# Two column-half scatter chains in place of one row scatter chain, in an attention and mixture-of-experts kernel

## The reference, cut to what matters

```python
buf_tok = jnp.full((E, CAP), T, jnp.int32).at[sorted_e, pos].set(sorted_tok, mode='drop')  # E=64, CAP=128
gx = xp[buf_tok]                                          # up to 128 tokens for each expert
gu = jnp.einsum('ech,ehi->eci', gx, gate_up_proj)         # 512 -> 2*192
g, u = jnp.split(gu, 2, axis=-1)
hid = jax.nn.silu(g) * u
eo = jnp.einsum('eci,eih->ech', hid, down_proj) * buf_w[..., None]   # 192 -> 512
routed = jnp.zeros((T + 1, h), x.dtype).at[buf_tok.reshape(-1)].add(eo.reshape(-1, h))[:T]
shared = jax.nn.silu(xf @ shared_gate_w.T) * (xf @ shared_up_w.T) @ shared_down_w.T
x = x + routed + shared
```

## Times and profile before

| quantity | us |
|---|---|
| time, median of 3 runs | 708.5 |
| lowest and highest of them | 704.78, 715.64 |
| time of the profiled execution | 706.73 |
| span of its profile, first to last instruction | 705.0 |
| TensorE matmul busy | 584.1 |
| VectorE busy | 230.0 |
| POOL busy | 246.5 |

### The profile page before, as it was taken

The page is one execution under the profiler, slowest core; times in us unless marked ns, Lnnn a source line. Parts: engine busy times, 40 slices in busy tenths (PEclk is TensorE's granted clock), DMA queues, the critical chain, the costliest instruction groups (busy, mean ns, idle before and its releaser), DMA issues.

```text
span 705.0 us, 6326 instructions
## 1 busy us (share of the span) xinstructions
PE 584.1 (83%) x2035; PEld 312.2 (44%) x2035; DVE 230.0 (33%) x572; ACT 173.0 (25%) x352; POOL 246.5 (35%) x235
## 2 busy tenths in 40 slices
PE   5999827777799999999999997999789998964810
PEld 2444314554445555555555553555345554532400
DVE  3866724863832222222132221222212222220210
ACT  4577733365101111121111111111011121110100
POOL 1145573353141333343323424333233333324220
PEclk9999959778989999999999999999979999996965
DMA  8935434489134989999998897997968898987432
GB/s 231 242 131 105 42 109 158 170 257 280 60 108 132 272 222 272 251 268 268 248 263 230 223 261 202 263 262 218 255 158 252 245 269 267 241 208 198 101 45 34
DMA packets 68953, 141.44 MB, mean 201 GB/s; under 512 B 13553, under 2 KB 16113, under 8 KB 68913
## 3 DMA queue, kind: packets, MB, share of 16 engines
q1 hardware_dynamic: 48240, 93.22, 42.7%
q0 software_dynamic: 18032, 43.54, 30.2%
q10 hardware_dynamic: 2640, 4.20, 1.7%
HBM read 107.89 MB, written 33.04 MB: 200 GB/s over the span
## 4 chain that ended last, share of the span: by engine, by line
DMA 43%; PE 28%; issue 12%; DVE 5%; ACT 4%; POOL 4%; SPq 1%; POOLq 0%; ACTq 0%; DVEq 0%
DMA out<-y,table 38%; PE bank L773 8%; PE bank L652 6%; PE bank L761 5%; DMA out<-x 5%; PE bank L666 3%; PE bank L575 2%; ACT rows L844 1%; PE bank L753 1%; SPq L319 1%; POOL picked L416 1%; DVE ones_lo L1082 1%; POOL x L425 1%; DVE ones_hi L1078 1%; DVE s L1003 1%
## 5 line engine op out<-in xcount | busy, mean ns | idle before, releaser
L501 POOL DMA_INDIRECT out<-y,table x64 | 101.4, 1584 | 294.8 <-DMA out<-y,table 213.2
L773 PE MATMUL bank<-gu_w,gxT 128*128 128x384 f32 x512 | 176.6, 488 | 0.8 <-ACT gxT L945 0.8
L761 PE MATMUL bank<-dn_w,hidT 96*128 96x512 f32 x256 | 126.7, 618 | 1.0 <-DVE hidT L1216 1.0
L1199 DVE TENSOR_SCALAR y<-bank,gx 128x512 f32<-128x512 f32 x64 | 48.1, 751 | 225.1 <-PE bank L761 208.9
L773 PEld LDWEIGHTS bank<-gu_w,gxT 128*128 128x128 f32 x512 | 93.0, 192 | 52.2 <-issue 1.6
L953 ACT ACTIVATE eg<-bank 128x192 f32<-128x192 f32 x64 | 21.2, 331 | 287.5 <-PE bank L773 287.5
L652 PE MATMUL bank<-xnT,upT 128*128 128x512 f32 x192 | 91.3, 620 | 0.0
L1211 DVE TENSOR_TENSOR hid<-bank,eg 128x192 f32<-128x192 f32 x64 | 31.8, 497 | 130.1 <-ACT eg L953 130.1
L753 PE MATMUL bank<-ident,gx 128*128 128x128 f32 x256 | 40.9, 284 | 36.9 <-DMA gx<-rows_dram,table 36.9
L507 POOL DMA_INDIRECT gx<-rows_dram,table x64 | 63.6, 994 | 21.7 <-issue 18.9
L761 PEld LDWEIGHTS bank<-dn_w,hidT 96*128 96x128 f32 x256 | 47.7, 197 | 48.5 <-issue 47.1
(11 more groups left out here) (164 smaller groups left out, 464.9 us busy)
## 6 DMA issues: line engine op xcount, KB each, us to landing
gu_w<-in_gate_up SPq DMA_DIRECT2D x128, 384.0 KB, 4.3
dn_w<-in_down SPq DMA_DIRECT2D x128, 192.0 KB, 5.8
x<-in_x SPq DMA_DIRECT2D x4, 1024.0 KB, 9.3
feat_dram<-feat SPq DMA_DIRECT2D x16, 256.0 KB, 3.1
rows_dram<-rows ACTq DMA_DIRECT2D x4, 1024.0 KB, 4.8
out<-x SPq DMA_DIRECT2D x4, 1024.0 KB, 5.7
out<-x POOLq DMA_DIRECT2D x3, 1024.0 KB, 10.4
w<-in_W SPq DMA_DIRECT2D x5, 256.0 KB, 7.7
```

What stands on the lines that cost most here:

```text
L501: pool.indirect_dma_start(a["out"][:, :], bass.IndirectOffsetOnAxis(ap=table[:, e:e + 1], axis=0), y[:, e % YB, :], None, compute_op=ALU.a ...
L761: last = nc.tensor.matmul(DN[:], hidT[:, e % 2, j, :], dn_w[:, e % U, j, :], start=(j == 0), stop=(j == 1))
L773: last = nc.tensor.matmul(GU[e % 2][:, 0:2 * I], gxT[:, e % 2, c, :], gu_w[:, e % U, c, :], start=(c == 0), stop=(c == KC - 1))
L1199: nc.vector.tensor_scalar(y[:, e % YB, :], DN[:], gx[:, e % GX, D + e:D + e + 1], None, ALU.mult).then_inc(y_ready, 1)
```

## The change

The output is viewed as 4096 rows of 256 columns, so that row 2t is the left half of token t and row 2t+1 the right half. Each expert's scatter becomes two, `scatter(e, 0)` and `scatter(e, 1)`, with 128 rows of 256 columns each. Each half has a semaphore of its own, so the left halves wait only for left halves and the right ones for right ones. The three `add_shared` wait for both halves, and both halves wait for them. The addresses of the halves are made on VectorE beside `table`.

```diff
-                def scatter(e):
+                def scatter(e, h):
                     pool.wait_ge(y_ready, e + 1)
-                    if chain_before(e):
-                        pool.wait_ge(added, 16 * chain_before(e))
-                    pool.indirect_dma_start(a["out"][:, :], bass.IndirectOffsetOnAxis(ap=table[:, e:e + 1], axis=0),
-                                            y[:, e % YB, :], None, compute_op=ALU.add).then_inc(added, 16)
+                    if e:
+                        pool.wait_ge(half_added[h], 16 * e)
+                    if shared_before(e):
+                        pool.wait_ge(shared_added, 16 * shared_before(e))
+                    pool.indirect_dma_start(halves, bass.IndirectOffsetOnAxis(ap=half_at[:, h, e:e + 1], axis=0),
+                                            y[:, e % YB, h * (D // 2):(h + 1) * (D // 2)], None,
+                                            compute_op=ALU.add).then_inc(half_added[h], 16)
...
                 for e in range(E):
-                    scatter(e)
+                    scatter(e, 0)
+                    scatter(e, 1)
                     if e + GX < E:
                         gather(e + GX)
-                    if e + 1 < E and chain_before(e + 1) > chain_before(e) + 1:
-                        pool.wait_ge(added, 16 * (chain_before(e) + 1))
-                        add_shared(chain_before(e + 1) - (e + 1))
+                    if e + 1 < E and shared_before(e + 1) > shared_before(e):
+                        for h in range(2):
+                            pool.wait_ge(half_added[h], 16 * (e + 1))
+                        add_shared(shared_before(e + 1))
...
-                nc.vector.scalar_tensor_tensor(table[:], spare2[:], -1.0, POS[:, LIST], ALU.add, ALU.add).then_inc(table_ready, 1)
+                link(nc.vector.scalar_tensor_tensor(token_of[:], spare2[:], -1.0, POS[:, LIST], ALU.add, ALU.add))
+                nc.vector.tensor_copy(table[:], token_of[:]).then_inc(table_ready, 1)
+                nc.vector.tensor_scalar(half_at[:, 0, :], token_of[:], 2.0, None, ALU.mult)
+                nc.vector.tensor_scalar(half_at[:, 1, :], token_of[:], 2.0, 1.0, ALU.mult, ALU.add).then_inc(halves_ready, 1)
...
                     if e >= YB:
-                        dve.wait_ge(added, 16 * (chain_before(e - YB) + 1))
+                        for h in range(2):
+                            dve.wait_ge(half_added[h], 16 * (e - YB + 1))
```

More of the change, by code:

```diff
@@ L130, in main_block @@
         table = sb("table", [P, E], U32)
+        half_at = sb("half_at", [P, 2, E], U32)
+        token_of = sb("token_of", [P, E])
         spare = sb("spare", [P, E])
@@ L226, in main_block @@
         g_in = [sem(f"eg_in{u}") for u in range(GX)]
-        gT_done, gxT_ready, gu_done, eg_ready, hid_ready, hT_done, hidT_ready, dn_done, y_ready, added = (
+        gT_done, gxT_ready, gu_done, eg_ready, hid_ready, hT_done, hidT_ready, dn_done, y_ready, shared_added = (
             sem(s) for s in ("egT_done", "gxT_ready", "gu_done", "eg_ready", "hid_ready",
-                             "hT_done", "hidT_ready", "dn_done", "y_ready", "added"))
+                             "hT_done", "hidT_ready", "dn_done", "y_ready", "shared_added"))
+        half_added = [sem(f"half_added{h}") for h in range(2)]
+        halves_ready = sem("halves_ready")
         bank = k.psum
@@ L274, in whole_batches, with shared_before @@
             return first_unit(e) // units
-        def chain_before(e):
-            return e + (whole_batches(e - 2) if e >= 2 else 0)
-        links = E + B - 1
+        def shared_before(e):
+            return whole_batches(e - 2) if e >= 2 else 0
+        halves = a["out"].rearrange("t (h d) -> (t h) d", h=2)
         ahead = [4, 6, 8, 9, 10, 11, 12, 13, 14, 15, 16] + [NT] * 6
@@ L494, in add_shared @@
                     pool.dma_start(a["out"][b * N:(b + 1) * N, :].rearrange("(t p) d -> p t d", p=P),
-                                   k.x[:, b * TB:(b + 1) * TB, :], accum_op=ALU.add).then_inc(added, 16)
-                def scatter(e):
+                                   k.x[:, b * TB:(b + 1) * TB, :], accum_op=ALU.add).then_inc(shared_added, 16)
+                def scatter(e, h):
                     pool.wait_ge(y_ready, e + 1)
-                    if chain_before(e):
-                        pool.wait_ge(added, 16 * chain_before(e))
-                    pool.indirect_dma_start(a["out"][:, :], bass.IndirectOffsetOnAxis(ap=table[:, e:e + 1], axis=0),
-                                            y[:, e % YB, :], None, compute_op=ALU.add).then_inc(added, 16)
+                    if e:
[5 more added lines that the diff above has]
+                                            compute_op=ALU.add).then_inc(half_added[h], 16)
                 def gather(e):
@@ L517, in _ @@
                 pool.wait_ge(x3_out, 16)
+                pool.wait_ge(halves_ready, 1)
                 for e in range(E):
-                    scatter(e)
+                    scatter(e, 0)
+                    scatter(e, 1)
                     if e + GX < E:
                         gather(e + GX)
-                    if e + 1 < E and chain_before(e + 1) > chain_before(e) + 1:
-                        pool.wait_ge(added, 16 * (chain_before(e) + 1))
-                        add_shared(chain_before(e + 1) - (e + 1))
-                pool.wait_ge(added, 16 * links)
+                    if e + 1 < E and shared_before(e + 1) > shared_before(e):
[3 more added lines that the diff above has]
+                for h in range(2):
+                    pool.wait_ge(half_added[h], 16 * E)
+                pool.wait_ge(shared_added, 16 * (B - 1))
             @block.tensor
```

## The result

The changed kernel takes 701.0 us, median of 20 runs (695.1 to 709.3); the kernel before took 709.6 in 20 runs beside it. The ratio is 0.987 with a 95% interval of 0.984 to 0.989: 1.3% faster, where 666 us was forecast and 698 was the upper end of the range. That is under the 2% that the prediction took as the least a measurement of this kernel can tell, and its chance for that was 0.12. Some executions of any kernel here are in a slower state, and the ratios leave them out. The profiled execution has a span of 699.7 us, 35 above the walk's 664.7.

The account below looks back on a forecast made before the run. TensorE bounds up to 350 us, then the serial chain of scatters. Scatter 19 at 354.0, 6.0 us periods, 19.3 us additions, 45.7 us for nine last steps and the end give span 664.7, time 666.4 us; range 648 to 698.

Parts of the forecast that it names:

- the walk: Sum of POOL's scatter starts along the left chain, from scatter 19 at 354.0 us to a span of 664.7 us.
- What bounds the kernel: TensorE up to 350 us, then the serial chain of scatters, 7.2 us each in the middle.
- POOL's price: POOL's descriptor writing for a half scatter, priced like a whole one at 1.58 us; 5.05 us for an expert.
- A row of 1 KB: In the scatter's transfer, a 1 KB row costs some 44% less than a 2 KB one.
- A half link in the clear: One half scatter without load: 0.85 us saved, landing after 4.1 us, link 4.9 us.
- The loaded period: Time per expert between shared additions under load: 7.2 us less 1.2 us of transfer, so 6.0 us.
- Shared additions: Step from the scatter ahead of each to the one behind: 19.3 us instead of 18.3, as both halves must land.
- Up to scatter 19: TensorE leads the chain; scatter 19 starts at 354.0 us, 0.5 us later through the added address work on VectorE.
- TensorE's stalls: Gathers stand behind scatters up to 15 us late; TensorE stalls only near the end, off the path.
- The halves only queue behind each other: Rival: shared DMA engines make a half land no sooner than a whole; 685 to 713 us, chance 0.15.
- TensorE becomes the bound: Rival: loaded period falls to POOL's 5.05 us, chain level with TensorE; 659 or 653 us, chance 0.13.
- The fixed row cost: Rival: a scatter's row costs 0.27 us whatever its bytes; about 740 us (over 715), chance 0.08.

## Why the prediction was wrong, point by point

- **What bounds the kernel.** Right up to 350 us, and right that the chain of accumulations is never idle behind it. What I left out is that the DMA engines were near their limit at the same time. I named their share (0.87 and 0.89) and used it against a rival, but the 0.87 hides a change: from 212 to 235 us the share is 0.57, and from 235 on it is 0.92.
- **POOL's price.** Right: 1567 ns for 1.58 us forecast.
- **A row of 1 KB.** Right: in 6 us that hold nothing but halves, 322 packets, 45 of them small ones, so 277 rows, took 39.3% of 16 engines' time, 136 ns for a row with the small packets' time in it; a whole row took 0.27 us, and 44% less is 0.15. The DMA view of the kernel after from 686 to 692 us:

```profile
DMA packets 322, 0.28 MB, mean 47 GB/s; under 512 B 45, under 2 KB 322, under 8 KB 322
...
q0 software_dynamic: 322, 0.28, 39.3%
```

- **A half link in the clear.** 3.8 us to land, forecast 4.1; the last nine steps 46.5, forecast 45.7. The Trainium skill's fit ("DMA: Bandwidth & Descriptors", the SWDGE path's anatomy) would have saved 0.3 us on a landing; the trace shows 1.0 to 1.2.
- **The loaded period: the step that failed.** The forecast said "the loaded period becomes 7.2 - 1.2 = 6.0 us". It read the longer landings under load as the scatter's own transfer, stretched, of which a half would save its share. The runs show that they come from the other transfers. Without the weights a whole scatter lands after 4.8 us instead of 6.4; with them the half saves only 0.6 us of landing and 0.5 of the period, which is 6.7 us. Without them both chains are level with TensorE again by expert 36. The rows to suspect it stood there: the shares of 0.87 and 0.89. By the estimate above an expert asks each engine for 6.2 to 6.5 us, so the walk's 6.0 asked for more than all their time. That estimate supports the cause; the runs without and with half of the loads are what shows it.
- **Shared additions.** 22.1 and 23.8 for 19.3, 19.4 for the third. The three transfers took 11.5 to 14.1 us where they took 9.1 to 12.3, and the pair must have landed before each. Undersized by 7.3 us in sum. Without the weight loads they were 16.3, 16.3 and 17.2, which points at the same load.
- **Up to scatter 19.** Forecast as untouched but for 0.5 us. Scatter 19 was 4.4 us behind its y, where it was 0.3 behind; with the engines at 0.96 the two chains began to fall behind already at TensorE's pace. The 0.5 us itself is there: TensorE's L678 waits 0.44 us for the shared product.

```profile
198.88 12.25 PE L678 MATMUL bank<-downT,shid 128*128 128x512 f32 x24 [0.44 <-DVE shid L1123]
```

- **TensorE's stalls.** I had them "only near the end". They are 35.8 us, for 36.9 before, and begin at 383. The lag behind the first addition, 21.5 us, is longer than the 15 I allowed.
- **The rivals.** "The halves only queue behind each other" had 0.15 and 685 to 713 us; it is close to what happened, and its argument (shared engines, 0.87 to 0.89 busy) is the cause found. Its "a half lands no sooner than a whole" is too strong: a half landed 0.6 us sooner. The Trainium skill's rule behind it ("DMA: Bandwidth & Descriptors", rules for kernel authors) says of halves by partition that they serialize; for these column halves, in chains where each link waits for the one before, a gain of 1.3% was left under full load. "TensorE becomes the bound" is how the kernel without loads behaves, at 658 us, for the 659 worked out there. The fixed row cost is ruled out.

## What to carry to other kernels

Before shortening a chain of transfers, multiply its period by the DMA share, in a stretch that holds nothing else. That estimates the engine time that one period asks for, and a forecast period near or below it is in doubt. It is rough, because the share can pass 1 and the time of the same packets changes with the load. With the share above 0.9, a second chain in flight gave 1.3% here, and half as much weight traffic gave about 6%. A landing time read under load isn't a price of the transfer alone: the part that other transfers add doesn't shrink with its size.

## What the runs showed of the hardware

- Landing against load isn't a straight line: 4.8, 5.0 and 6.4 us for a whole scatter with none, half and all of the weight loads (shares of 0.47, 0.75 and 0.92 from 235 to 350 us).
- The DMA share can pass 1 (1.03 from 400 to 420 us in the kernel after, at 284 GB/s), and the packets of one queue took 46.5% or 37.4% of it for nearly the same bytes.
- POOL writes 128 descriptors of an accumulating scatter in 1.57 us whether a row has 2048 or 1024 bytes, and those of a gather in 1.0.
- The end is not cut much by halves: from the last left half to the end of the span 14.1 us pass, as with the last whole scatter, since the right half follows 1.9 us behind.
